# Gated cross-attention and ternary FFN on one core: storing places, turnings and one ternary moved before the loop, and tile 3's scores ahead of tile 1's attention on TensorE

## The reference, cut to what matters

```python
# x (4, 2048, 512), ctx (4, 77, 384); 8 heads of 64; FFN 512 -> 2048 -> 512; all f32
def attention(x, ctx, Wq, Wk, Wv, Wo, bo):
    q, k, v = x @ Wq, ctx @ Wk, ctx @ Wv                 # split into 8 heads
    attn = softmax(q @ k.T / 8, axis=-1)                 # 77 keys for each head
    return concat_heads(attn @ v) @ Wo + bo
def act_quant(x):    # to integers of -128..127, by row
    s = 127 / clip(max(abs(x), -1), 1e-5); return round(x * s) / s
def weight_quant(w): # to -1, 0, 1, by the mean magnitude of the whole matrix
    s = 1 / clip(mean(abs(w)), 1e-5); return clip(round(w * s), -1, 1) / s
def ffn(x, w_gate, w_up, w_down):
    g, u = act_quant(x) @ weight_quant(w_gate).T, act_quant(x) @ weight_quant(w_up).T
    return act_quant(relu(g) ** 2 * u) @ weight_quant(w_down).T
x = x + tanh(g_xattn) * attention(layernorm(x), ctx, Wq, Wk, Wv, Wo, bo)
x = x + tanh(g_ffn) * ffn(layernorm(x), w_gate, w_up, w_down)
```

## Time and profile before

| | us |
|---|---|
| median of three runs | 1192.87 |
| the profiled execution | 1192.44 |
| its span in the profile | 1190.6 |
| PE / DVE / ACT / POOL busy | 1170.7 / 1034.7 / 870.4 / 300.1 |
| mean granted TensorE clock | 0.997 of full speed |

### The profile page before, as it was taken

How to read it: one execution, slowest core, us unless ns; L and a number is a source line. 1 busy time by engine, 2 the same in 40 slices (tenths; PEclk the granted TensorE clock), 3 DMA queues, 4 the chain that set the end, 5 groups by cost and what they waited for, 6 DMA issues and landing times.

```text
span 1190.6 us, 18823 instructions
## 1 busy us (share of the span) xinstructions
PE 1170.7 (98%) x5851; PEld 740.8 (62%) x5851; DVE 1034.7 (87%) x2124; ACT 870.4 (73%) x929; POOL 300.1 (25%) x301
## 2 busy tenths in 40 slices
PE   9979999999999999999999999999999999999998
PEld 7546656666665666566566656666665666566554
DVE  4988898888988888888998888889899888988887
ACT  5877777776887777677877767776787777677764
POOL 3121222222442222222442222222244222222200
PEclk9999999999999999999999999999999999999999
DMA  9873554443444464444444464443444444444333
GB/s 375 279 255 81 149 145 108 98 110 92 100 115 101 118 164 112 97 106 101 101 99 101 114 172 115 97 110 93 101 112 102 99 97 113 98 105 100 87 66 71
DMA packets 289780, 144.69 MB, mean 122 GB/s; under 512 B 254651, under 2 KB 258063, under 8 KB 287569
## 3 DMA queue, kind: packets, MB, share of 16 engines
q1 hardware_dynamic: 289741, 144.32, 47.4%
q10 hardware_dynamic: 4, 0.00, 0.0%
HBM read 57.86 MB, written 24.35 MB: 69 GB/s over the span
## 4 chain that ended last, share of the span: by engine, by line
PE 87%; DVE 4%; DMA 3%; ACT 2%; SPq 2%; issue 2%; POOL 0%; DVEq 0%; ACTq 0%
PE gu_ps L1110 34%; PE o_ps L1074 18%; PE y_ps L1124 17%; PE s_ps L68 17%; DMA staged<-in_wg_t 2%; SPq L522 1%; DVE half_max L1365 1%; DVE staged L1359 1%; DMA a_scr<-a_spare 1%; DMA hq_t<-staged 0%; PE gu_ps L1243 0%; ACT staged L800 0%; DVE pt_low L1348 0%; PE gu_ps L1212 0%; DVE prob_sum L1341 0%
## 5 line engine op out<-in xcount | busy, mean ns | idle before, releaser
L1110 PE MATMUL gu_ps<-w_up,xq_t 128*128 128x512 bf16 x1024 | 241.9, 379 | 1.9 <-DVE staged L1359 1.8
L1110 PE MATMUL gu_ps<-w_gate,xq_t 128*128 128x512 bf16 x1016 | 240.9, 380 | 1.5 <-DMA xq_t<-xq 1.0
L1124 PE MATMUL y_ps<-w_down,hq_t 128*128 128x512 bf16 x1008 | 228.0, 379 | 0.5 <-DMA hq_t<-staged 0.5
L1074 PE MATMUL o_ps<-v_sb,pt_high 128*128 128x512 f32 (+1 forms) x640 | 214.7, 416 | 6.3 <-DVE pt_low L1348 6.3
L1359 DVE TENSOR_TENSOR staged<-staged,gu_ps 128x1024 f32<-128x1024 f32 x128 | 155.6, 1215 | 54.2 <-ACT staged L806 54.2
L68 PE MATMUL s_ps<-a_sb,xf_high 128*128 128x308 f32 x1024 | 187.4, 305 | 0.0
L1110 PEld LDWEIGHTS gu_ps<-w_up,xq_t 128*128 128x128 bf16 x1024 | 99.8, 98 | 123.8 <-DVE staged L1359 3.8
L846 ACT ACTIVATE staged<-staged,h_scale 128x1024 f32<-128x1024 f32 x126 | 137.9, 1142 | 48.5 <-DVE h_scale L1379 48.5
L1124 PEld LDWEIGHTS y_ps<-w_down,hq_t 128*128 128x128 bf16 x1008 | 98.7, 98 | 119.6 <-DMA hq_t<-staged 1.0
L670 POOL TENSOR_TENSOR rstd<-var_eps,neg_half 128x1 f32<-128x1 f32 x128 | 95.8, 748 | 304.5 <-DVE var_eps L1324 275.6
L800 ACT ACTIVATE staged<-gu_ps 128x1024 f32<-128x1024 f32 x127 | 129.1, 1016 | 52.1 <-PE gu_ps L1110 52.0
(11 more groups left out here) (155 smaller groups left out, 1421.0 us busy)
## 6 DMA issues: line engine op xcount, KB each, us to landing
xf_sb<-in_x_feat SPq DMA_DIRECT2D x64, 256.0 KB, 2.6
x_sb<-in_x_tok SPq DMA_DIRECT2D x64, 256.0 KB, 2.8
y<-staged SPq DMA_DIRECT2D x63, 256.0 KB, 2.1
staged<-in_wg_t SPq DMA_DIRECT2D x4, 1024.0 KB, 18.1
folded<-a_scr SPq DMA_DIRECT2D x3, 1232.0 KB, 6.2
staged<-in_wd_t SPq DMA_DIRECT2D x3, 1024.0 KB, 8.5
folded<-v_scr SPq DMA_DIRECT2D x3, 1024.0 KB, 5.7
w_up<-in_wu_t SPq DMA_DIRECT2D x2, 1024.0 KB, 16.2
```

The lines of the kernel that those rows point to most:

```text
L1074: last = nc.tensor.matmul(o_ps[:, :], pt[0:rows, P * c:P * (c + 1)], v_sb[0:rows, v, c, :], start=(c == 0 and pt is pt_high and v == 0), s ...
L1110: last = nc.tensor.matmul(target[:, q, :], xq_t[:, s.par(0), c, :], w[:, c, cols], start=(c == 0), stop=(c == DC - 1))
L1124: last = nc.tensor.matmul(y_ps[:, :], hq_t[:, c, :], w_down[:, c, :], start=(c == 0), stop=(c == FC - 1))
```

## The change: what it does

It touches the prologue and step 0 only; the loops are the same.

- **Places.** Place 3 becomes the whole of `bo_sb` (now 128 partitions), place 4 the tile `planes_t`, seen as f32. Every place is now 512 contiguous columns in a partition, and a DMA is written as whole rows. Parts 0 to 9 go round five places, parts 10 to 15 round four (places 0 to 3), so that place 4 is free after part 9. `turn_probs` of tile 1 writes `planes_t`, and waits for part 9's store first.
- **SP.** `turn_probs(1)` and `store_keys(3, 2)` move ahead of the stores of parts 11 and 12.
- **ACT.** `part_probs(1)` moves ahead of `measure(2, 1)`; `measure(2, 3)` goes to DVE; `exponentials(2)` moves behind `join_probs(1)` and `probs_high(1)`.
- **DVE.** `sum_probs(1)` moves ahead of `ternary(1, 2)`; `measure(2, 3)` comes in behind `measure(2, 2)`; at the end of the prologue the order is `scale(2, 0)`, `probs_low(1)`, `scale(2, 1)`, `ternary(2, 1)`, `sum_probs(2)`. `ternary(2, 0)` moves into step 0, where `top_half(0)` and `ternary(2, 2)` now stand behind `hidden_half(1)`.
- **PE.** In step 0 tile 3's scores stand ahead of tile 1's attention.

```diff
-V_OUT_RING = 5
+V_PLACES = 5
+V_PLACE = [k % V_PLACES if k < 2 * V_PLACES else (k - 2 * V_PLACES) % (V_PLACES - 1) for k in range(16)]
-        bo_sb = sb("bo_sb", [1, DIM], F32)
+        bo_sb = sb("bo_sb", [P, DIM], F32)
-        v_slots = [x1[:, 1 + n, :].rearrange("p (q n) -> p q n", q=HP) for n in range(QUAD - 1)]
-        v_slots += [k_pairs[:, :, b, 0:P] for b in range(2)]
+        v_slots = [x1[:, 1 + n, :] for n in range(QUAD - 1)] + [bo_sb[:, :], planes_t[:, :, :].rearrange("p c n -> p (c n)").bitcast(F32)[:, 0:DIM]]
...
                     wait(sp, probs_joined, s.before(d - 1))
+                    if s.opens(1 - d):
+
+                        wait(sp, v_stored[V_PLACES - 1], 32 * V_PLACE.count(V_PLACES - 1))
                     sp.nop(nofuse=True)
                     sp.dma_start_transpose(planes_t[:, :, :], planes[:, :]).then_inc(probs_turned, 16)
...
-                        sp.dma_start(v_scr[b, at + j:at + j + n, :].rearrange("p (q n) -> p q n", q=HP),
-                                     v_slots[k % V_OUT_RING][r:r + n, :, :]).then_inc(v_stored[k % V_OUT_RING], 16)
+                        sp.dma_start(v_scr[b, at + j:at + j + n, :],
+                                     v_slots[V_PLACE[k]][r:r + n, :]).then_inc(v_stored[V_PLACE[k]], 16)
...
                 turn_input(start, 0)
+                turn_probs(start, 1)
+                store_keys(3, 2)
                 store_later_values(11)
                 store_later_values(12)
-                turn_probs(start, 1)
-                store_keys(3, 2)
                 store_later_values(13)
...
-                    if k >= V_OUT_RING:
-
-                        act.wait_ge(v_stored[k % V_OUT_RING], 32 * (k // V_OUT_RING))
+                    if k >= V_PLACES:
+
+                        act.wait_ge(v_stored[V_PLACE[k]], 32 * V_PLACE[:k].count(V_PLACE[k]))
...
                 take_later_values(12)
+                part_probs(start, 1)
                 measure(2, 1)
-                part_probs(start, 1)
                 high_part(start, 3)
                 take_keys(3, 2)
                 take_later_values(13)
-                measure(2, 3)
                 take_keys(3, 3)
                 take_later_values(14)
                 take_later_values(15)
-                exponentials(start, 2)
                 join_probs(start, 1)
                 probs_high(start, 1)
+                exponentials(start, 2)
...
                         gate_up(s, 0)
+                    if s.opens(0):
+                        make_scores(s, 3)
                     if s.has(1) and s.has(3):
                         attend(s, 1)
-                    if s.has(3):
+                    if s.has(3) and not s.opens(0):
                         make_scores(s, 3)
...
                     shift_scores(s, 3)
+                    ternary(2, 0, w_down)
+                    hidden_half(s, 1)
+                    probs_low(s, 2)
                     top_half(s, 0)
                     ternary(2, 2, w_down)
-                    hidden_half(s, 1)
-                    probs_low(s, 2)
                     ternary(2, 3, w_down)
...
+                sum_probs(start, 1)
                 ternary(1, 2, w_up)
-                sum_probs(start, 1)
                 dve.wait_ge(rstd1_done, 2)
                 input_stats(start, 2)
                 measure(2, 2)
+                measure(2, 3)
                 sum_rows(2)
...
                 scale(2, 0)
-                sum_probs(start, 2)
+                probs_low(start, 1)
                 scale(2, 1)
                 ternary(2, 1, w_down)
-                probs_low(start, 1)
-                ternary(2, 0, w_down)
+                sum_probs(start, 2)
```

More of the change, by code:

```diff
@@ L279, in gated_block @@
         a_stored = [sem(f"a_stored{n}") for n in range(A_RING)]
-        v_stored = [sem(f"v_stored{n}") for n in range(V_OUT_RING)]
+        v_stored = [sem(f"v_stored{n}") for n in range(V_PLACES)]
         a_high_done, a_split_done = sem("a_high_done"), sem("a_split_done")
@@ L436, in load_values @@
                     sp.wait_ge(bias_stored, 16)
-                    for n in range(V_OUT_RING):
-                        sp.wait_ge(v_stored[n], 32 * len(range(V_LATER)[n::V_OUT_RING]))
+                    for n in range(V_PLACES):
+                        sp.wait_ge(v_stored[n], 32 * V_PLACE.count(n))
                     full = (KC - 1) * P
@@ L779, in take_later_values @@
                     act.wait_ge(vo_done, KC + k + 1)
-                    if k >= V_OUT_RING:
-                        act.wait_ge(v_stored[k % V_OUT_RING], 32 * (k // V_OUT_RING))
-                    nc.scalar.activation(v_slots[k % V_OUT_RING][0:rows, :, :],
-                                         value_slots[(KC + k) % V_RING][0:rows, :].rearrange("p (q n) -> p q n", q=HP), ACT.Copy,
+                    if k >= V_PLACES:
+                        act.wait_ge(v_stored[V_PLACE[k]], 32 * V_PLACE[:k].count(V_PLACE[k]))
+                    nc.scalar.activation(v_slots[V_PLACE[k]][0:rows, :], value_slots[(KC + k) % V_RING][0:rows, :], ACT.Copy,
                                          scale=gate_tanh[0:rows, 0:1]).then_inc(vo_taken, 1)
@@ L899, in gate_bias @@
                     act.wait_ge(bo_loaded, 16)
-                    nc.scalar.activation(bias_row, bo_sb[:, :], ACT.Copy, scale=gate_tanh[0:1, 0:1]).then_inc(bias_gated, 1)
+                    nc.scalar.activation(bias_row, bo_sb[0:1, :], ACT.Copy, scale=gate_tanh[0:1, 0:1]).then_inc(bias_gated, 1)
                     act.wait_ge(bias_gated, 1)
@@ L971, in _ @@
                 act.dma_start(gate_row[:, :], gates).then_inc(gates_loaded, 16)
-                act.dma_start(bo_sb[:, :], bo).then_inc(bo_loaded, 16)
+                act.dma_start(bo_sb[0:1, :], bo).then_inc(bo_loaded, 16)
                 take_key_pairs(0)
@@ L1388, in add_attention @@
                         if s.opens(n + 1 - d):
-                            wait(dve, v_stored[n], 32 * len(range(V_LATER)[n::V_OUT_RING]))
+                            wait(dve, v_stored[n], 32 * V_PLACE.count(n))
                     here = x1[:, s.ring(d), :]
```

## The result

The changed kernel took **1198.16 us** in the median of 5 runs (1197.56 to 1198.67), against 1192.4 of the kernel before on the same chip: a ratio of 1.0048 (95%: 1.0035 to 1.0062), so it is slower by more than the 0.2% that can be told. The forecast was 1194.9, with a range up to 1197.2: right in sign, 3.3 us short, and missed by the range. The profiled execution took 1198.2 us for a span of 1196.3 (before: 1192.44 and 1190.6).

A forecast was written before the change was run, and what follows sets the result against it. The VectorE and ScalarE chain was taken to set when tile 5's attention starts, after which TensorE never idles. The terms summed to +2.05 us at h_scale(0): 1192.44 + 2.05 = 1194.5, with 0.43 for the median 1194.9; range 1192.0 to 1197.2.

The forecast's parts named there:

- the store of part 11: Prologue: second DMA issued at 77.4, landing 3.0 us later at 80.4, so take_later_values(15), ready at 79.85, waits 0.6 us.
- costs nothing: Prologue, SP's new wait on part 9's store: issued by 66, SP comes to it at 73.5, so no cost.
- The likeliest case: The forecast itself for the whole kernel: slower by 0.8 to 3.2 us, chance 0.57.
- Clearly slower: SP's queue: Rival, prologue: part 11 landing after 79.85 delays join_probs(1) one for one; +3.3, or +5 with part 9 late; chance 0.16.
- Step 0 on VectorE: From unmark_input(1) to the end of h_scale(0): 2.5 us longer, 1.87 for ternary(2, 0) and 0.65 beside POOL's low part.
- The exclusion of POOL's normalise: Prologue, tile 1: the ternary's first pass shuts out POOL's normalise(1), which ends 1.08 us later at 72.2.
- The folding later: Prologue: 1.85 us later, behind measure(2, 1); take_keys(3, 2) at 75.9, not 74.03, and fold_keys(3, 3) at 76.6, not 74.75.
- Attention at full clock behind the scores: Step 0, TensorE: tile 3's scores run to 86.85, tile 1's attention to 90.35 at full clock, without 5.46 us of idleness.
- the sum as a whole: All terms together: +2.05 us at h_scale(0), carried unchanged to tile 5's attention near 162.4.
- TensorE does not bind: Step 1: TensorE waits some 7 us, restarts at 0.50; tile 2's attention 1 to 2 us late, at most as VectorE.

The follow-up runs named there:

- d1_before_split: The kernel before with the later values cut into parts of 122 and 109 rows instead of 116 and 115: 1191.61 us (0.9997).
- c3_split: The kernel after with the later values cut into parts of 122 and 109 rows instead of 116 and 115: 1194.93 us (1.0022).
- a2_measure_first: The kernel after with measure(2, 1) ahead of part_probs(1) on ScalarE, as before: 1197.22 us (1.0037).
- d3_split_measure: The kernel after with parts of 122 and 109 rows and measure(2, 1) ahead of part_probs(1): 1193.66 us (1.0009).
- b1_scores_first: The kernel before with tile 3's scores ahead of tile 1's attention in step 0 on TensorE: 1193.0 us (1.0003).
- d2_before_split_scores: The kernel before with parts of 122 and 109 rows and tile 3's scores ahead of tile 1's attention: 1192.69 us (0.9998).
- a5_ternary_back: The kernel after with ternary(2, 0) moved from step 0 back into the prologue, between scale(2, 0) and probs_low(1): 1196.69 us (1.0033).

## Why the prediction was wrong, and where it was right

**The step that failed** is the store of part 11, "0.6 us of wait", with the sentence that the new wait on part 9's store "costs nothing". `take_later_values(15)` was forecast for 80.4 and came at 84.30. By the chain after, the second DMA of part 11 was issued at 79.38 and not 77.4 (+1.98), and landed in 4.84 us and not 3.0 (+1.84): together 3.82 of the 3.90. (Both times count from the start of the second DMA's issue.) Of the 1.98, some 1.2 are SP still at the late turning when the key copy was done at 77.04, about 0.5 the start of this execution (`add_attention(0)` began 0.58 later than before), and the rest slower issues.

Both sizes came from one error. I took the landing from rows of key stores, 2.8 us at least, because SP's queue was empty there; but the key stores, of 128 rows, are not cut like the value stores. The row to go by was the 5.35 us issue in the earlier trace rows. I read it as a cost of stores out of `k_pairs` that goes when the buffer is contiguous. `d1_before_split`, still out of `k_pairs`, shows it gone with 32 rows instead of 38, and the kernel after, with contiguous buffers, shows it turned into 10.69 us of flight. It was in part a backlog of DMAs of 38 rows: with 32 rows part 9 still took 7.90 us, and what holds it then is not shown (two loads of 1024 KB for `w_down` are issued 4 us ahead of it). But in `c3_split` SP comes to the turning only at 74.0, so 7.90 cost nothing; in the kernel after it is free at 75.0 and has to wait till 76.7. The estimate from the Trainium skill ("DMA: Bandwidth & Descriptors", section "Anatomy of one DMA"), 2.4 us with 2.0 fixed and bytes by rate, by which nothing would have waited, was further off than the row for the kernel after, and close to the 2.49 of `c3_split`; that section fits it to DMAs issued by GpSimd, and these are SP's.

**The likeliest case was the wrong one.** "Clearly slower: SP's queue" named the mechanism, its place and its point, with part 9 late too: +5. I gave it 0.16; +5.76 was measured. Its price for part 11 was the median of the earlier trace rows, 4.3, close to the 4.84; what it lacked was a row for part 9 in flight.

**Unforeseen, but without a price of its own**: TensorE idles 2.00 us ahead of `fold_keys(3, 3)`, the clock is 0.50 from 77 to 87 us, and the four matmuls behind take 3.76 us (1.97 in `a2_measure_first`). The total came at 83.14 and `scale(2, 0)` at 84.28, not 81.0. `a2_measure_first` removes this and gains nothing, so it ran beside the store. With the stores mended it comes next: the runs of `c3_split` fall in two groups, 1193.73 to 1194.83 us at a mean clock of 0.996, and 1195.04 to 1197.05 at 0.993 or 0.994. `d3_split_measure`, whose folding isn't late, has only two of eleven at 0.994 (1194.67 and 1194.75). That the upper group is the slow folding is likely from this and not shown: the profile of `c3_split` is of the lower one.

**Right** were the other terms, one of them by luck (below). Step 0 on VectorE: +2.52 forecast, +2.51 measured, with `ternary(2, 0)`'s first pass at 1.86 us beside POOL's low part and not 1.22. The exclusion of POOL's normalise: 2.10 us, from 70.66. The folding later: `take_keys(3, 2)` at 76.38 for 75.9, less the later start. Attention at full clock behind the scores, and no gain from it. In the kernel after, the chain from `h_scale(0)` to tile 5's attention carries a delay one for one: +5.72 at both ends. And the sum as a whole: with the stores' wait taken out, `c3_split` reaches tile 5's attention at 162.19 for 162.4. Its parts compensate a little: it starts about 0.5 late, its store lands in 2.49 and not 3.0, and VectorE idles 0.51 and not 1.2 us ahead of `probs_low(1)`.

"TensorE does not bind" holds in the kernel after and in `c3_split`, but not with much to spare. In `b1_scores_first` and `d2_before_split_scores` the chain goes over TensorE's late gate/up 1, and a gain of 0.50 and of 1.07 us at `h_scale(0)` is gone at tile 5's attention; in `a5_ternary_back` 1.51 of 1.81 get through. Had the other terms been smaller, the sum would have had to price this.

**The +2.5 of step 0 was right in size and not in its parts.** The prediction puts all of it on `ternary(2, 0)` and nothing on the new order, `hidden_half(1)` ahead of `top_half(0)` and `ternary(2, 2)`. `a5_ternary_back` has in step 0 the work of the kernel before in that new order, and takes 11.13 us for it, not 9.65: 1.48 us more, 1.38 of them VectorE's wait for `square_half`. The ternary fills this wait in the kernel after and adds 1.03 to it. So about 1.5 us belong to the order and 1.0 to the ternary; no run has the order of before with the ternary in it. (`h_scale(0)` of `a5_ternary_back` is at 111.94 for 113.75; the other 0.8 stood already at `join_probs(1)`, 84.09 for 84.89, and 0.53 of it at `add_attention(0)`.)

## What to carry to other kernels

When a change makes an engine or a queue wait for a store, price that store from a row of the same cut and the same backlog, not from the shortest row of another tensor; and read an issue that takes six times its median as a store that is late, which a new wait will inherit. Look at the row counts of DMAs: in the kernel after, 38 and 39 rows in place of 32 and 45 cost some 3.2 us, more than the 2.2 that all the reordering costs without them. In the kernel before the better cut gained nothing that could be told, since VectorE's list came next. An idle stretch of TensorE is worth what the engine behind it gains: of 5.46 us taken away here, none came through. And a piece of work that fills another wait costs less than its length; look for that wait before blaming the piece.

## What the runs showed of the hardware that was not expected

- The time of a store went by the number of rows of the smaller DMA more than by its bytes. Part 11's second DMA, 77 rows each time, landed 2.49 us after the start of its issue behind one of 32 rows (64 KB), 4.84 behind 38 (76 KB), and 6.59 behind 37 (74 KB); part 9's, in a backlog, 7.90, 10.69 and 14.33.
- The backlog shows in either of two places. With the place in `k_pairs` SP's two issues take 6.30 us; with contiguous `planes_t` they take 0.60 and the flight is 10.69. With 37 rows the issues out of `planes_t` are slow as well, 5.18 us.
- The semaphore of a store goes up in as many steps as the rule on engines gives, for all 16 parts: 2 + 11 with 38 and 77 rows, 16 + 11 with 32 and 77, 1 + 11 with 37 and 77.
- Where TensorE's clock falls varies between kernels that do the same work there: 0.72 over 68 to 74 us in `c3_split` (after 1.50 us of idleness from 66.7) with full clock from 77 to 87, but 1.00 and 0.50 in the kernel after. Part of a difference of 1 or 2 us between single executions is this, so the sums above are compared event by event.
